# Own-engine waits as drains: a graph attention layer with a mixture of experts on one core

## The reference

```python
def gnn(x, src, dst, W, a_src, a_dst):            # H = 4 heads of 64
    h = einsum('nf,hfo->nho', x, W)
    scores = leaky_relu(e_s[src] + e_d[dst], 0.2) # e_s, e_d: h times a_src, a_dst
    ex = exp(scores - segment_max(scores, dst)[dst])
    alpha = ex / maximum(segment_sum(ex, dst)[dst], 1e-9)
    return relu(segment_sum(alpha * h[src], dst)).reshape(N, 256)

def ffn(x, gamma, beta, Wr, br, W1, b1, W2, b2):  # 8 experts, the best 2 of each node
    xn = layernorm(x) * gamma + beta
    w = softmax(top_k(xn @ Wr + br, 2))
    return sum over the chosen e: w[e] * (gelu(xn @ W1[e] + b1[e]) @ W2[e] + b2[e])

x = x + gnn(layernorm(x), ...)
x = x + ffn(layernorm(x), ...)
```

## Time and profile before

| | |
|---|---|
| median of 3 runs | 1389.72 us (1388.78 to 1392.36) |
| the profiled execution | 1383.32 us, its span 1381.5 us |
| DVE busy | 747.7 us (54%), 1860 instructions |
| POOL busy | 770.1 us (56%), 821 instructions |
| PE busy | 711.3 us (51%), 2540 matmuls |
| ACT busy | 429.5 us (31%), 1137 instructions |
| granted PE clock, mean | 0.742 |

### The profile page before, as it was taken

The page is one execution under the profiler, slowest core; times in us unless marked ns, Lnnn a source line. Parts: engine busy times, 40 slices in busy tenths (PEclk is TensorE's granted clock), DMA queues, the critical chain, the costliest instruction groups (busy, mean ns, idle before and its releaser), DMA issues.

```text
span 1381.5 us, 11297 instructions
## 1 busy us (share of the span) xinstructions
PE 711.3 (51%) x2540; PEld 532.8 (39%) x2540; DVE 747.7 (54%) x1860; ACT 429.5 (31%) x1137; POOL 770.1 (56%) x821
## 2 busy tenths in 40 slices
PE   0630114544535453555445544544456567999990
PEld 0520113333423342344324432333334454676770
DVE  6511325564556555655555555646657785444445
ACT  3440204332433243324422442233324253222220
POOL 6467766666666666666766676666660003444430
PEclk9965557777676777667766776677678658999995
DMA  8344433333333333333333333333338221122117
GB/s 294 124 99 111 107 89 84 94 92 98 96 98 97 102 88 98 96 94 96 99 93 96 96 100 88 96 97 95 96 89 275 76 76 46 62 66 65 65 47 234
DMA packets 78788, 142.20 MB, mean 103 GB/s; under 512 B 22113, under 2 KB 50243, under 8 KB 78595
## 3 DMA queue, kind: packets, MB, share of 16 engines
q0 software_dynamic: 38992, 108.47, 28.2%
q1 hardware_dynamic: 37147, 30.44, 7.0%
q10 hardware_dynamic: 2584, 2.56, 0.6%
HBM read 125.57 MB, written 16.48 MB: 103 GB/s over the span
## 4 chain that ended last, share of the span: by engine, by line
issue 30%; DVE 21%; PE 17%; PEldq 14%; PEld 12%; another core or an unknown queue 3%; DMA 1%; ACT 1%; SPq 1%; DVEq 1%; POOL 0%; POOLq 0%; ACTq 0%
PEldq L640 13%; PEld psum L638 12%; PE psum L728 6%; PE psum L750 6%; DVE acc L1130 3%; PE psum L740 1%; PE psum L588 1%; DVE links L1160 1%; DVE C L1170 1%; DVE ring L1217 1%; PE psum L680 1%; PE psum L717 1%; DVE TB L1179 1%; DVE TB L1183 1%
## 5 line engine op out<-in xcount | busy, mean ns | idle before, releaser
L530 POOL DMA_INDIRECT ring<-h_tab,srcP x664 | 631.1, 950 | 311.5 <-issue 194.6
L638 PE MATMUL psum<-ring,shared 128*128 128x260 f32 x1328 | 440.3, 500 | 486.0 <-issue 430.2
L638 PEld LDWEIGHTS psum<-ring,shared 128*128 128x128 f32 x1328 | 330.3, 256 | 585.4 <-issue 454.0
L1130 DVE TENSOR_TENSOR acc<-acc,psum 128x260 f32 x332 | 140.4, 423 | 307.0 <-PEq L640 252.2
L844 ACT ACTIVATE shared<-iota_f,Dcol 128x128 f32<-128x128 f32 x664 | 202.2, 386 | 174.5 <-PEq L640 159.2
L1217 DVE TENSOR_TENSOR ring<-ring,psum 128x2048 f32<-128x2048 f32 x83 | 189.8, 2287 | 27.1 <-remote 24.6
L862 ACT ACTIVATE Ex<-Z 128x128 f32<-128x128 f32 x21 | 6.5, 309 | 463.8 <-issue 267.5
L540 POOL DMA_INDIRECT ring<-z_tab,ring x47 | 45.4, 967 | 136.3 <-DVEq L1430 122.3
L849 ACT ACTIVATE shared<-shared,ones 128x1024 f32<-128x1024 f32 x83 | 95.3, 1148 | 28.0 <-remote 21.7
L946 ACT ACTIVATE RS_all<-psum,tail_consts 128x128 f32<-128x128 f32 x188 | 53.6, 368 | 145.7 <-PE psum L740 145.7
L546 POOL DMA_INDIRECT ys_tab<-shared,ring x47 | 45.8, 975 | 94.2 <-DVE shared L1453 94.2
(11 more groups left out here) (293 smaller groups left out, 677.9 us busy)
## 6 DMA issues: line engine op xcount, KB each, us to landing
ring<-h_tab,srcP POOLq DMA_INDIRECT x664
ring<-in_L_ffn_W SPq DMA_DIRECT2D x16, 512.0 KB, 9.7
h_tab<-ring SPq DMA_DIRECT2D x10, 260.0 KB
ring<-in_x SPq DMA_DIRECT2D x1, 2432.0 KB
z_tab<-ring SPq DMA_DIRECT2D x2, 1024.0 KB, 4.4
ring<-ys_tab SPq DMA_DIRECT2D x4, 512.0 KB, 9.0
ring<-ys_tab ACTq DMA_DIRECT2D x4, 512.0 KB, 9.8
out<-acc SPq DMA_DIRECT2D x4, 512.0 KB
```

The lines of the kernel that those rows point to most:

```text
L530: pool.indirect_dma_start(out=ring[:, t % RING, :], out_offset=None, in_=h_tab, in_offset=bass.IndirectOffsetOnAxis(ap=srcP[:, t:t + 1], a ...
L638: pe.matmul(sums[G_at % NSUM][:, 0:MW], dst_oh[:, n % OHB, 2 * g + r, :], ring[:, t % RING, :], start=(r == 0), stop=(r == 1))
L1130: v.tensor_tensor(a, a, sums[(n * GB + g) % NSUM][:, 0:MW], ALU.add).then_inc(flushed, 1)
```

## The change

Each wait of DVE or ACT for a semaphore that the same engine counts up becomes a drain: the engine's sequencer holds back what follows until the engine has finished all that it was given. The instructions no longer count up `s_dve`, `squared` and `lane_squared`, and these three semaphores are gone; `flushed`, `gates_made` and the others are still counted up, since other engines wait for them. No other instruction is changed, added or moved.

```diff
-    def __init__(self, eng, sem):
-        self.eng, self.sem, self.done, self.trip, self.per_trip, self.base = eng, sem, 0, 0, 0, 0
+    def __init__(self, eng):
+        self.eng = eng

     def link(self, ins):
-        self.done += 1
-        ins.then_inc(self.sem, 1)
-        self.eng.wait_ge(self.sem, self.done + self.trip * self.per_trip)
...
+        self.eng.drain()
...
                 for k in range(BT):
                     t = n * BT + k
-                    last = act.activation(dst_oh[:, n % OHB, k, :], iota_f[:, :], ACT.Square, scale=-1.0,
+                    act.activation(dst_oh[:, n % OHB, k, :], iota_f[:, :], ACT.Square, scale=-1.0,
                                           bias=Dcol[:, t:t + 1])
-                last.then_inc(squared, 1)
-                act.wait_ge(squared, n + 1)
+                act.drain()
...
-                last.then_inc(lane_squared, 1)
-                act.wait_ge(lane_squared, n // 2 + 1)
+                act.drain()
...
             v.tensor_scalar(flags, flags, 1.0, BIG, ALU.subtract, ALU.mult).then_inc(flags_made, 1)
-            v.wait_ge(flags_made, 1)
-            v.wait_ge(spos_ready, 1)
+            v.drain()
             v.nop().then_inc(early_over, 1)
...
                     v.tensor_tensor(a, a, sums[(n * GB + g) % NSUM][:, 0:MW], ALU.add).then_inc(flushed, 1)
-                    v.wait_ge(flushed, n * GB + g + 1)
+                    v.drain()
...
-                v.wait_ge(gates_made, f + 1)
+                v.drain()
...
                 v.tensor_scalar(fac[:, :], soft[:, 0:H], 1.0, None, ALU.add).then_inc(fac_used, 1)
-                v.wait_ge(fac_used, f)
+                v.drain()
...
-                v.wait_ge(x1_made, n + 1)
+                v.drain()
...
                  .then_inc(table_in, 1)
-                v.wait_ge(table_in, n + 1)
+                v.drain()
```

More of the change, by code:

```diff
@@ L284, in gat_moe_kernel @@
         assert used[0] <= RING * MW, used
-        s_const, s_pool, s_dve = sem("s_const"), sem("s_pool"), sem("s_dve")
+        s_const, s_pool = sem("s_const"), sem("s_pool")
         x_in, w_in, a_in, ends_in = (sem(n) for n in ("x_in", "w_in", "a_in", "ends_in"))
@@ L316, in gat_moe_kernel @@
         z_ready, ex_ready = sem("z_ready"), sem("ex_ready")
-        squared, oh_made = sem("squared"), sem("oh_made")
+        oh_made = sem("oh_made")
         weighed, batch_done, flushed = sem("weighed"), sem("batch_done"), sem("flushed")
@@ L328, in gat_moe_kernel @@
         x_again_in = [sem(f"x_again_in{n}") for n in range(len(SETS))]
-        lanes_known, lane_squared, lanes_made = (sem(n) for n in ("lanes_known", "lane_squared", "lanes_made"))
+        lanes_known, lanes_made = (sem(n) for n in ("lanes_known", "lanes_made"))
         z_stored, table_in, table_done, where_ready = (
@@ L929, in _ @@
                 for i in range(n * CH, (n + 1) * CH):
-                    last = act.activation(lane_oh[:, i, :], iota_f[:, :], ACT.Square, scale=-1.0,
+                    act.activation(lane_oh[:, i, :], iota_f[:, :], ACT.Square, scale=-1.0,
                                           bias=lane32[:, i:i + 1])
-                last.then_inc(lane_squared, 1)
-                act.wait_ge(lane_squared, n // 2 + 1)
+                act.drain()
                 of = lane_oh[:, n * CH:(n + 1) * CH, :].rearrange("p i n -> p (i n)")
@@ L967, in _ @@
         def _(v):
-            c = Chain(v, s_dve)
+            c = Chain(v)
             v.memset(xs0[:, NB - 1, :], 0.0).then_inc(pads_set, 1)
```

## The result

The change makes the kernel slower: 1402.44 us, the median of 4 runs (1398.88 to 1403.86), against 1390.01 (1388.78 to 1392.36) for the kernel before on the same chip. The ratio is 1.0081, 95% interval 1.0069 to 1.0093, so 11 to 12 us more. I had forecast 1394.8, slower, with a range of 1376 to 1410. The sign and the range were right.

A forecast was written before the change was run, and what follows sets the result against it. No engine is full in the loop; the gathers' pace, 1.42 us each, sets it. 142 exposed drains x 0.09 = +12.8, less 7.7, is +5.1 us: 1388.4 profiled, plus 6.4 to the median, 1394.8; range 1376 to 1410.

The forecast's parts named there:

- If a drain wakes up at its usual time, the gathers start 7.7 us earlier: Preparation, on the path: 8 late waits between L1046 and L1052 add 7.7 us, which drains would remove.
- rival 2: DVE's drain held like PE's: first form 1402.5, without the 7.7 us gain; second, longer POOL stops, 1465; chance 0.15.
- Loop, cost nothing: Loop: 688 drains, 62 us of DVE time, covered by the gathers' pace and DVE's 252.2 us idle; zero.
- DVE's late waits fall where PE's drain is held anyway: Loop: late waits come near the end of a run of gathers, so removing them gains nothing.
- The price of a drain, 0.09 us: One DVE drain against a queued wait of 0.035 us: 0.09 us more, bounds 0.02 and 0.20.
- The count in routing, 47: Routing, 1131.5 to 1152.3 us: 47 of 52 instructions end in a wait, all exposed, at 0.09 us each.
- The stretch behind the last gather, 45 x 0.09 = 4.1 us: 1032.9 to 1095.2 us: 17 in the last weights chain, 24 flush adds and 4 others exposed.
- ACT's drains, nothing: ACT's 85 drains: at most 17 us, covered as ACT runs 1 to 3 batches ahead, idle 267.5 us; zero.
- The first phase, nothing: Weights chain, 136.4 to 146.2 us: seven late waits, 7.3 us; gain costed at nothing, as POOL stops for gathers.
- About 0.15 us a gather: Loop: POOL's stop grows with the run of gathers before it, 13.1 us behind 88, 3.1 us behind 16.
- Rival 1, relief: About 670 updates fewer unload the queue that makes updates late: -23 us, about 1372; chance 0.22.
- Rival 3, waits cost nothing either way: Lateness reappears at the next wait for another engine, drains cost what waits did: 1389.7, or 1382.0; chance 0.18.

The follow-up runs named there:

- prep_only: Kernel before with drains in DVE's preparation alone (up to early_over), semaphore waits behind it; ratio to before 1.0025.
- counted: Changed kernel, but the instructions still count up s_dve and only the waits are drains; ratio to before 1.0127.
- pe_counts: Kernel before with PE's drain after each batch taken away, the batch's last matmul counting up batch_done itself; ratio to before 0.9987.
- fewer_waits: Kernel before with five links fewer in the preparation, and a batch's last matmul counting up batch_done in place of PE's drain; ratio to before 1.0003.
- after_again: The changed kernel measured once more, unaltered, on the second chip; ratio to the kernel before 1.0117.
- gathers_waits: Kernel before with 20 gathers of POOL added beside the routing chain, DVE's semaphore waits kept; ratio to before 1.0050.
- act_only: Kernel before with ACT's 85 waits as drains, DVE as before; ratio to before 1.0002.
- dve_only: Kernel before with DVE's waits for its own semaphores as drains, ACT keeping its two semaphores; ratio to before 1.0127.
- no_prep: Changed kernel with semaphore waits again in the preparation, drains (ACT's included) from the first phase on; ratio to before 1.0093.

## Why the prediction was right, and where it was not

- **"If a drain wakes up at its usual time, the gathers start 7.7 us earlier": the step that failed.** Drains were held where waits had been late: from the statistics to the first normalised row the five executions with drains took 14.2 to 20.3 us, the nine with waits 8.8 to 13.8. The preparation lost about 4 us instead of winning 5.4. I had this as rival 2, and discounted it with "it is the update that comes late on DVE, and most of its drains have none". prep_only and counted show that a drain needs no update to be held.
- **Loop, cost nothing.** Failed by 5 to 8 us. The cover of DVE's idle time was real for the plain price: 688 drains at 0.04 us are 28 us, 1.3 a phase. It covers longer chains of weights as well, up to the 260.7 us that they come to in pe_counts. It does not cover the one to five times in a kernel with drains when a held drain makes PE's batch itself later than the gathers' pace allows (1.1 to 3 us each time). "DVE's late waits fall where PE's drain is held anyway" held for the waits, and not for those drains.
- **The price of a drain, 0.09 us (bounds 0.02 and 0.20).** Mis-sized: 0.038 to 0.040 measured. I took the flush's gap as the nearest row, on the same engine but with a register operation in it; the other end, the drain at the end of the block, gave 0.02 and was the nearer one. The Trainium skill, "VectorE: DVE Perf Modes", section "The DRAIN you can't avoid", says that a semaphore costs nothing extra over the pipe's own emptying; a drain in a semaphore's place is another comparison, and the runs here put 0.04 us between the two.
- **The count in routing, 47.** Too low: the exposed chain begins at 1124.8 in the kernel before, not at 1131.5, and 60 waits end in it. 60 x 0.038 gave +2.3, and the whole stage +2.6, against +4.6 forecast for both stages behind the last batch.
- **The stretch behind the last gather, 45 x 0.09 = 4.1 us.** The size came out (+4.4 and +5.3 us within the two groups that can be compared), but by luck: 45 at 0.04 are 1.8. The rest is not attributed. It may be held drains, but this stretch alone takes 59.0 to 63.4 us in kernels without a drain of DVE in it.
- **ACT's drains, nothing.** Right: 1.0002. The experts, untouched: right.
- **The first phase, nothing.** Right for the time, though its chain of weights grew from 15.4 to 17.8 us in place of shrinking: POOL's stop behind the first 88 gathers went from 13.1 to 13.6 us.
- **"About 0.15 us a gather", read from the stops.** That is 13.1/88; behind a run of 16 it is 3.06/16 = 0.19. Nothing in the sum hung on it.
- **Rival 1, relief.** Refuted by counted: with the 586 counts kept or gone, the time is the same.
- **Rival 2's first form** was priced at 1402.5, which is the measured 1402.4. That is chance: its +12.8 us were 142 x 0.09, and at the true price they are 5.7; held drains make up most of the rest.
- **Rival 3, waits cost nothing either way.** Half right: in fewer_waits the lateness did reappear at the next wait, of the same engine. But a drain was not as cheap as a wait.

So the forecast was right in sign and range for a reason that it had weighed at 0.15, the held drains, while its own terms erred both ways: a gain of 7.7 us that never came, and a price more than twice too high.

Put together by stages on the second chip, after_again against the kernels there whose stage is that of before: 3.5 us in the preparation (the time of prep_only), 5.2 in the gathers (951.9 against 946.7), 4.4 behind the last one, 2.6 in routing, 0.8 in the combination. That is 16.5 us, and after_again has 1.0117, or 16.2, with an interval of 13 to 19. Of the 16.5, 151 exposed drains (26, 45, 60 and 20) at 0.04 us are 6.0; the other 10 are held drains as far as they are explained at all. The stages are taken from the same traces, so the sum shows that nothing large is missing, and not the cause of each part.

## What to carry to other kernels

Where an engine must wait for its own result, a semaphore wait that stands on the next instruction is the cheapest way in this kernel; a drain costs 0.04 us more each time in the best case, so count the links that are exposed before swapping one for the other. The waits that were late beside POOL's indirect DMAs were no cost of the semaphore: neither a drain nor fewer waits got around it. Moving the chain away from the gathers is what is left to try; no kernel here did. And a chain that grows is a loss only where its result comes later than everything else that the next step waits for: look for the stops that end right behind their releaser. An estimate that assumes a different instruction would not meet the same delay has to name what the delay is; PE's held drain stood in the trace of before as a warning.

## What the runs showed of the hardware that I had not expected

A count can arrive 3.4 us after the matmul that sends it has ended (PE to DVE in gathers_waits, 1.7 us behind the last gather; 0.2 us in act_only, which has no gathers there), and it is late whether a drain or a matmul sends it (pe_counts). Gathers keep a pace of 1.42 us each (34.1 us for 24, 22.8 for 16; up to 23.1 for 16 in other kernels) though each shows as 0.95 us on POOL. The Trainium skill, "Perfetto Trace Analysis", section "DMA Instruction — SWDGE (GPSIMD)", says that such a row ends when the last descriptor has been written, not when the data has moved; the trace agrees as far as it can: the row is 0.95 us long at a pace of 1.42.

DVE's drain can be held for 7.7 us behind the last operation (31.07 to 38.73 in the profile after) and not at all in another kernel that has the same instructions there (dve_only). Two engines can be let go together: in no_prep a drain of DVE and one of ACT, behind operations that had ended at 723.18 and 722.48 us, both end at 725.26. In act_only even rows that wait for nothing, the normalisations L1050, start on the same beat:

```profile
43.64 0.41 DVE L1050 TENSOR_SCALAR ring<-ring 128x256 f32<-128x256 f32 x1 [1.17 <-issue]
45.04 0.41 DVE L1050 TENSOR_SCALAR ring<-ring 128x256 f32<-128x256 f32 x1 [0.99 <-issue]
```

Each of them counts up a semaphore for PE. What ties this beat of 1.40 us to DVE was not found.
